# A cond-modulated FFN on one core: weights' loads, group 1's order on TensorE and VectorE

## The reference

```python
q_emb = relu(q @ W3 + b3)
x1 = (n * x + sum_over_tokens(x)) * q_emb[:, None, :]
y = relu(x1 @ W2 + b2)
base = y @ W_base + b_base
shared = (y @ A_s) @ B_s
gates = softmax(y @ W_router + b_router); w_per_e = top 2 of 6, the rest 0
hw = (y @ A_r[e]) * w_per_e[e]
out = x + base + shared + sum_e hw[e] @ B_r[e]
```

## Time and profile before

| what | value |
|---|---|
| median of the runs | 237.95 us |
| profiled execution: its own time | 237.04 us |
| its span, first to last instruction | 235.2 us |
| outside the span | 1.84 us |
| PE busy | 229.3 us (97% of the span) |
| DVE busy | 166.7 us (71%) |
| ACT busy | 86.2 us (37%) |
| POOL busy | 49.0 us (21%) |
| granted TensorE clock | 1.000 over the whole span |
| PE's share of the chain that ended last | 87% |

### The profile page before, as it was taken

The page is one execution under the profiler, slowest core; times in us unless marked ns, Lnnn a source line. Parts: engine busy times, 40 slices in busy tenths (PEclk is TensorE's granted clock), DMA queues, the critical chain, the costliest instruction groups (busy, mean ns, idle before and its releaser), DMA issues.

```text
span 235.2 us, 3088 instructions
## 1 busy us (share of the span) xinstructions
PE 229.3 (97%) x1006; PEld 186.9 (79%) x1006; DVE 166.7 (71%) x309; ACT 86.2 (37%) x171; POOL 49.0 (21%) x57
## 2 busy tenths in 40 slices
PE   7999899999999999999999999999999999999994
PEld 3977687788888888888888888888888888888883
DVE  0794997798979967497838969299665976064344
ACT  3369451534136330444206340263305351252330
POOL 6288422012132211023012120022111130000000
PEclk9999999999999999999999999999999999999999
DMA  6999903527053632717044541709020370104004
GB/s 214 340 219 227 253 4 71 142 99 261 11 137 65 222 137 37 175 70 289 8 117 89 187 172 22 185 4 329 28 33 0 126 231 13 22 0 178 3 0 178
DMA packets 32505, 28.80 MB, mean 122 GB/s; under 512 B 5817, under 2 KB 22909, under 8 KB 32494
## 3 DMA queue, kind: packets, MB, share of 16 engines
q1 hardware_dynamic: 30682, 28.50, 42.4%
q10 hardware_dynamic: 1812, 0.17, 0.6%
HBM read 18.89 MB, written 8.39 MB: 116 GB/s over the span
## 4 chain that ended last, share of the span: by engine, by line
PE 87%; SPq 6%; DVE 2%; DMA 2%; issue 0%; DVEq 0%
PE m_ps L747 78%; PE hT L747 9%; SPq L210 3%; DMA x_quart<-in_x_dram 2%; DVE out_nat L625 1%; SPq L226 1%; SPq L233 1%; SPq L229 1%; DVE xT L471 0%; SPq L231 0%; DVE vsum L476 0%; DVE x_sum L483 0%; SPq L237 0%; DVE y_lo L497 0%; SPq L236 0%
## 5 line engine op out<-in xcount | busy, mean ns | idle before, releaser
L308 POOL TENSOR_TENSOR x_full<-x_sum,qT 128x512 f32<-128x512 f32 x28 | 32.4, 1156 | 136.7 <-DVE x_sum L483 136.7
L353 ACT ACTIVATE y_hi<-m_ps,condT 128x512 fp32r<-128x512 f32 x32 | 21.9, 686 | 80.4 <-PE m_ps L747 80.2
L747 PE MATMUL m_ps<-Wb_lo,y_hi 128*128 128x512 f32 x128 | 49.8, 389 | 0.0
L747 PE MATMUL m_ps<-Wb_hi,y_hi 128*128 128x512 f32 x128 | 49.8, 389 | 0.0
L747 PE MATMUL m_ps<-Wb_hi,y_lo 128*128 128x512 f32 x128 | 49.8, 389 | 0.0
L747 PE MATMUL m_ps<-x_hi,W_hi 128*128 128x512 f32 x112 | 43.8, 391 | 0.0
L747 PE MATMUL m_ps<-x_hi,W_lo 128*128 128x512 f32 x112 | 43.6, 389 | 0.0
L747 PE MATMUL m_ps<-x_lo,W_hi 128*128 128x512 f32 x112 | 43.6, 389 | 0.0
L497 DVE TENSOR_TENSOR y_lo<-m_ps,y_hi 128x512 fp32r<-128x512 f32 x32 | 21.7, 677 | 30.3 <-ACT m_ps L355 30.3
L471 DVE STREAM_TRANSPOSE xT<-x_quart 128x512 f32<-128x512 f32 x28 | 30.3, 1084 | 3.0 <-DMA x_quart<-in_x_dram 3.0
L747 PEld LDWEIGHTS m_ps<-Wb_hi,y_lo 128*128 128x128 f32 x128 | 24.0, 188 | 5.0
(11 more groups left out here) (99 smaller groups left out, 255.1 us busy)
## 6 DMA issues: line engine op xcount, KB each, us to landing
out_dram<-out_nat SPq DMA_DIRECT2D x32, 256.0 KB, 2.3
x_quart<-in_x_dram SPq DMA_DIRECT2D x28, 256.0 KB, 4.5
x_nat<-in_x_dram SPq DMA_DIRECT2D x7, 1024.0 KB, 6.2
gatesT<-wT SPq DMA_DIRECT2D x28, 48.0 KB
x_nat<-in_x_dram SPq DMA_DIRECT2D x4, 256.0 KB, 3.4
W_f<-in_L_cond_W_dram SPq DMA_DIRECT2D x4, 256.0 KB, 6.0
Wb_f<-in_L_ffn_W_base_dram SPq DMA_DIRECT2D x1, 1024.0 KB, 8.7
W_sb<-in_L_cond_W_dram SPq DMA_DIRECT2D x2, 256.0 KB, 4.2
```

Source lines behind the costliest of these rows:

```text
L308: nc.gpsimd.tensor_tensor(per_batch(x1_full[:, c, :]), per_batch(x1_sum[:, c, :]), qT[:, c, bass.ds(BG * g, BG)].unsqueeze(2).to_broadcast ...
L353: nc.scalar.activation(y_hi[:, m, :], m1_ps[m][:, :], ACT.Relu, bias=b2_sb[:, m:m + 1]).then_inc(y_hi_ready, 1)
L747: mm = nc.tensor.matmul(psum, lhsT, rhs, start=start and i == 0, stop=stop and i == len(terms) - 1)
```

## The change

The load order: the quarters of group 1 now go out ahead of W_base and of Wd's parts. The orders that follow:

- ACT in the head: the second relu of q comes ahead of the first W2 split, the fourth ahead of the second x_hi; Wb_hi comes ahead of Wd_hi. POOL makes Wd_lo between the second and the third Wb_lo.
- PE in group 0: the first chunk of `m1_first` does the fourth bank last among the x_hi products; one more idle matmul stands at the start and one more among the q products; for each chunk, `m2(0, k)` stands ahead of `h(0, k)`, and both wait for y_lo.
- PE in group 1: the first three banks are written by `m1_second`, which does all products of x_hi first (24 matmuls) and those of x_lo last (12).
- DVE in group 0: both last y_rest come ahead of chunk 2 of group 1's x, which now stands behind the gates.
- DVE in group 1: weigh, hw_rest and the first output add come ahead of the first y_rest and of group 2's first turn.
- ACT in group 1: hw_split comes first, and the four `pick` copies move there from group 0.

```diff
-    WARM_LOAD, WARM_W3, WARM_HALF, WARM_Q = 7, 1, 2, 1
+    WARM_LOAD, WARM_W3, WARM_HALF, WARM_Q = 8, 1, 2, 2
     assert ONE < SH and SH + R <= RO and RO + E * R == P and TT == KC and NG % 2 == 0 and NG >= 4
...
                 sp.dma_start(W2_f[:, c, :], W2.rearrange("(p c) n -> p c n", c=KC)[:, c, :]).then_inc(W2_loaded[c], 16)
+            load_quarters(1, 1)
             sp.dma_start(Wb_f[:, :, :], W_base.rearrange("(k p) d -> p k d", p=P)).then_inc(Wb_loaded, 16)
...
             load_A_r(sp, range(KC // 2, KC))
-            load_quarters(1, 1)
             sp.wait_ge(zeroed, 4)
...
                 W_rest(W2_lo[:, c, :], W2_f[:, c, :], W2_hi[:, c, :], W2_lo_ready)
-            pool.wait_ge(Wd_hi_ready, 1)
-            W_rest(Wd_lo[:, :, :], Wd_f[:, :, :], Wd_hi[:, :, :], Wd_lo_ready)
             for k in range(KC):
...
                 W_rest(Wb_lo[:, k, :], Wb_f[:, k, :], Wb_hi[:, k, :], Wb_lo_ready)
+                if k == 1:
+                    pool.wait_ge(Wd_hi_ready, 1)
+                    W_rest(Wd_lo[:, :, :], Wd_f[:, :, :], Wd_hi[:, :, :], Wd_lo_ready)
             scale(1, 0)
...
             q_relu(0)
+            q_relu(1)
             W2_split(0)
-            q_relu(1)
+            q_relu(2)
             x1_split_head(0)
-            q_relu(2)
+            q_relu(3)
             x1_split_head(1)
-            q_relu(3)
             W2_split(1)
...
             W2_split(3)
-            act.wait_ge(Wd_loaded, 16 * (2 + KC))
-            nc.scalar.activation(Wd_hi[:, :, :], Wd_f[:, :, :], ACT.Copy).then_inc(Wd_hi_ready, 1)
             x1_split_head(3)
...
                 nc.scalar.activation(Wb_hi[:, k, :], Wb_f[:, k, :], ACT.Copy).then_inc(Wb_hi_ready, 1)
+            act.wait_ge(Wd_loaded, 16 * (2 + KC))
+            nc.scalar.activation(Wd_hi[:, :, :], Wd_f[:, :, :], ACT.Copy).then_inc(Wd_hi_ready, 1)
             act.wait_ge(bias_loaded, 16)
...
+                if second:
+                    hw_split(slice(0, TG), g)
                 for m in range(KC):
                     relu(g, m, first)
-                    if m == 0 and not first:
+                    if m == 0 and not first and not second:
                         hw_split(slice(0, TG), g)
...
                     nc.scalar.activation(Wu_hi[:, :], Wu_f[:, :], ACT.Copy).then_inc(Wu_hi_ready, 1)
+                    split(0)
+                if second:
                     pick_round()
...
                 if first:
-                    split(0)
                     split(1)
...
                     y_rest(g, 1)
-                    sum_x(g + 1, 1)
+                    total(1)
                     y_rest(g, 2)
-                    add_sum(g + 1, 1)
                     y_rest(g, 3)
-                    turn(2)
-                    total(2)
                 elif second:
+                    weigh_before()
+                    hw_rest_before()
+                    add_x(g - 1, 1 - par, UP_TILES[:1], 0)
                     y_rest(g, 0)
-                    weigh_before()
                     turn(0)
+                    y_rest(g, 1)
                     total(0)
-                    hw_rest_before()
-                    y_rest(g, 1)
-                    turn(1)
-                    add_x(g - 1, 1 - par, UP_TILES[:1], 0)
                     y_rest(g, 2)
                     add_x(g - 1, 1 - par, UP_TILES[1:], 1)
+                    turn(1)
+                    y_rest(g, 3)
                     total(1)
                     rest(0)
-                    y_rest(g, 3)
                     rest(1)
...
                 if first:
-                    rest(0)
+                    turn(2)
+                    total(2)
                 if first or second:
...
                 if first:
+                    rest(0)
                     rest(1)
...
-                for k in range(KC // 2):
+                pe.wait_ge(x1_hi_ready, 1)
+                pe.wait_ge(W2_hi_ready, 1)
+                for m in range(KC - 1):
+                    pe.wait_ge(qT_ready, m + 1)
+                    chunk(m, 0, W2_hi, x1_hi)
+                pe.wait_ge(W2_lo_ready, 1)
+                for m in range(KC - 1):
+                    chunk(m, 0, W2_lo, x1_hi)
+                pe.wait_ge(qT_ready, KC)
+                chunk(KC - 1, 0, W2_hi, x1_hi)
+                chunk(KC - 1, 0, W2_lo, x1_hi)
+                pe.wait_ge(x1_lo_ready, 1)
+                for m in range(KC):
+                    chunk(m, 0, W2_hi, x1_lo)
+                for k in range(1, KC // 2):
                     pe.wait_ge(x1_hi_ready, k + 1)
...
                     for m in range(KC):
-                        if k == 0:
-                            pe.wait_ge(qT_ready, m + 1)
                         chunk(m, k, W2_hi, x1_hi)
...
+            def m1_second():
+                x_hi, x_lo = x1_hi[1], x1_lo[1]
+                for k in range(KC):
+                    pe.wait_ge(x1_hi_ready, KC + k + 1)
+                    for m in range(KC - 1):
+                        cols = slice(m * P, (m + 1) * P)
+                        product(m1_ps[m][:, :], [(W2_hi[:, k, cols], x_hi[:, k, :]),
+                                                 (W2_lo[:, k, cols], x_hi[:, k, :])], k == 0, False)
+                for m in range(KC - 1):
+                    cols = slice(m * P, (m + 1) * P)
+                    for k in range(KC):
+                        if m == 0:
+                            pe.wait_ge(x1_lo_ready, KC + k + 1)
+                        mm = product(m1_ps[m][:, :], [(W2_hi[:, k, cols], x_lo[:, k, :])], False, k == KC - 1)
+                    mm.then_inc(m1_done, 1)
             def h(g, k, first):
...
                 else:
-                    for m in range(KC - 1):
+                    if second:
+                        m1_second()
+                    for m in () if second else range(KC - 1):
                         m1(g, par, m)
...
                 for k in range(KC - 1):
+                    if first:
+                        pe.wait_ge(y_lo_ready, k + 1)
+                        m2(0, k, first)
                     h(g, k, first)
-                    if first:
-                        m2(0, k, first)
                 if not first:
...
```

## The result

The changed kernel took 244.49 us (median; 244.12 to 245.32) against 237.94 us (237.47 to 238.31): ratio 1.0281, 95% interval 1.0249 to 1.0313. It is 6.5 us slower. The direction and the place were forecast, the size was not: 3.65 us were forecast, and the range ended at 243.2.

What follows compares the result with a forecast made beforehand. PE, busy 97% of the span, was taken as the bound. Group 0's +0.7 us lies inside the +3.6 us at group 2, giving 241.6 us against 237.95; range 239.2 to 243.2.

Steps and rivals of the forecast that it cites:

- The second term: DVE in group 1 waits for up, runs 4.05 us later; PE's group 2 start slips +3.6 us, first term included.
- the exposed wait of POOL and ACT at rest(1): DVE, group 1: rest(1) directly behind total(1) exposes POOL's 1.25 and ACT's 0.63 us before x_lo 1.
- the gap itself: PE, first bank of group 2: a wait of about 3.4 us for x_lo, at 66 to 71.
- nothing is given back and nothing added: Later groups keep their order, DVE waiting for PE, so the time behind group 2's wait stays unchanged.
- The first term: Group 0: W_base landing at 19.3 delays ACT and DVE; group 1 starts at 38.55 instead of 37.87, +0.7 us.
- The head: ACT and PE changes before group 0 move m1_first's end by 0 to 0.5 us, costed at nothing.
- The first add: DVE, group 1: the first output add waits for up's first tile at 47.55 and starts from 47.6.
- The logits: DVE, group 1: their subtraction stays slow beside POOL's product, 0.7 us kept in the sum; without it +2.9.
- A: Loads: W_base and Wd land by 17.5, group 1 starts about 1.3 us earlier; +2.3, 240.3 us; chance 0.17.
- B: Loads: W_base lands at 21.05, every step after it 1.7 us later; +5.3, 243.3 us; chance 0.10.
- C: Group 2's first bank doesn't wait, only the gaps of groups 0 and 1 count; faster, 235.75 us; chance 0.08.
- D: Gains in the gaps are lost in the wait, no change within 0.2% (0.48 us); chance 0.07.

Runs made afterwards that it cites:

- e1: The changed kernel with group 2's first turn and total and its second turn put ahead of DVE's first output add in group 1: 238.24 us, ratio 1.0015.
- e5: The kernel before with only group 1's changes (x_hi products first on PE, hw_split first on ACT, new DVE order): 243.12 us, ratio 1.0219.
- e2: The changed kernel with 9 idle matmuls ahead of the third and 5 ahead of the fourth chunk of group 2's first bank: 242.35 us, ratio 1.0189.
- e2b: The changed kernel with 9 idle matmuls ahead of the third chunk of group 2's first bank, none ahead of the fourth: 242.40 us, ratio 1.0195.
- e4: The kernel before with only the new load order and the ACT and POOL weight splits that go with it: 238.15 us, ratio 1.0020.
- e10: e1 with the quarters' load back behind Wd: 238.35 us, ratio 1.0029.
- e3: The changed kernel with the quarters' load back behind Wd, all other orders still changed: 244.12 us, ratio 1.0254 (1.0181 to 1.0327).
- e8: The kernel before with only DVE's group 0 order changed, first y_rest ahead of the first turn, the others one place earlier: 237.93 us, ratio 1.0012.
- e6: The kernel before with e8's DVE order, group 1's changes as in e5 and DVE's wait filled as in e1: 236.53 us, ratio 0.9959.

## Why the prediction was wrong in size

- **The second term, DVE's chain in group 1: right.** The order exposed DVE's wait for up (about 3 us forecast, 3.38 measured), and the exposed wait of POOL and ACT at rest(1) was 1.60 us (1.88 forecast). e1 takes the wait away and the kernel is back at before; e5 adds it alone and has both gaps. Of the gap itself, 3.4 us were forecast, and 3.2 stand in the trace, in two parts as the text allowed.
- **The low clock: missing.** The sum took it that a gap costs its length once. It cost a second time: 1.75 us in the profiles, 2.1 us in the medians by e2 and e2b. This is the larger part of the 2.9 us by which the forecast fell short. In the profiles it fell short by 3.6: the 1.75, and 1.84 by which group 2's fourth chunk came behind the forecast 71.3 (73.14), which are 0.87 of the head, 0.39 of group 0 and about 0.5 of the first add. The failed step is the one that says of what lies behind the wait "nothing is given back and nothing added". The Trainium skill's page "TensorE: Matmul & The Clock Gate", section "Part 1: The HAM clock gate", says that the clock has two levels, 1.2 and 2.4 GHz, and follows how busy the engine was; the traces agree, with 1.00 up to the gaps, and behind them 0.57 over 4 us and matmuls at the pace of 1.2 GHz. By it this should have been a rival with a price.
- **The first term, group 0: right in kind, small in size.** W_base landed at 20.4, not 19.3; in the other kernels with this load order (e1, e2, e2b, e4) it landed at 19.7 to 20.4. The sum counted bytes and left out that its issue would stand behind the quarters' issues and take longer itself; how much of the 1.1 us that is, no run separates. ACT's relu started 1.0 us after the forecast 22.0. Group 1 started at 39.81, not 38.55: 0.87 of it is the head, 0.4 is group 0. The two waits that were forecast in group 0, 1.0 to 1.5 us and about 0.5, measured 1.45 and 0.54. But e10 and e4 show that the loads' move is not what made the kernel slower: the gap in front of the first m2 exists with either order.
- **The head, costed at nothing.** From the start of the q products to the first real product it is 3.97 us before and 4.40 now; kernels with the old head have 3.97 to 4.15, with the new one 4.22 to 4.40. About 0.3 us, inside the bound of 0.5. What of it reached the end was not separated from the scatter of the head.
- **The first add started 0.5 us late.** Its matmul ends at 48.8 (48.42 and 0.39), the add starts at 49.35; the first add of group 2 starts 0.11 us behind its matmul. It is no chance: e2, e2b, e3 and e5, where DVE waits for the same add, have 0.53 to 0.55. The sum had it start at once. The cause stays open.
- **The logits.** They took 0.87 us again (64.59 to 65.46), with POOL's product beside them (64.38 to 65.42), as the sum kept them.
- **Rivals.** A (early weights) is refuted by W_base at 20.4, B (late weights, 21.05) was nearer for the landing, C and D by the gaps. None of them priced the clock, and neither did the range.

## What to carry to other kernels

An engine far from busy on the average can still set the time by where it waits: before moving a waiting instruction up, look at what stood ahead of it and now queues behind it. When a change opens gaps of microseconds on TensorE, price them by their length, and hold a second price ready for the matmuls behind them at the lower clock: it was paid for two gaps close together here and not for a single one of 1.3 us, so the granted clock of that stretch is what to look at first. A gap that has two owners close together (here quarters and weights) did not shrink when the load of one was moved ahead of the other; it went when the instruction that PE waited for no longer queued behind the quarters (e8), and it paid only together with an order that did not want the next operand early (e6).

## What the runs showed of the hardware

- Two gaps of 1.92 and 1.31 us with three matmuls (1.0 us) between them were followed by matmuls 0.427 us apart up to 76.78, which is 1.2 GHz, and cost 2.1 us by the medians; one gap of 1.32 us behind idle matmuls was followed by none (e2b). In one of four executions of e3, with the same orders in group 1, the mean clock stayed at 1.000. A gap of 0.95 and one of 0.47 us in e8 left the pace of the matmuls behind them near 0.23 us as well.
- The four quarter loads of 256 KB took 3.04 us to issue with W2's load still under way, and W_base's 1 MB 2.80 us behind them, where the same issue took 0.44 us before. Two loads of A_r, 48 KB each, took 5.98 us to issue before and 5.20 now. So the time of an issue on this queue is no measure of the load's bytes; what sets it was not tested.
- The start of the real work differs by up to 0.7 us between profiles of kernels with the same head (first q product 7.28 to 8.02 us; in the latest of them, e4, PE waited 0.54 us for x). A difference of that size between two profiles shows nothing by itself.
- DVE's addition of x's sum (128x512) took 0.69 us by itself and 1.46 to 1.80 us in e3, e10 and e4, where it ran while POOL made Wb_lo.
